# Third batch's shared down products moved to the closing stage, expert weights loaded in paced parts, odd sums as two additions

## What is computed

```python
h = _layernorm(x) * (1 + ca) + sa
x = x + ga * attention(h)                 # 16 heads of 16
h = _layernorm(x) * (1 + cb) + sb
# router: softmax over 32 experts, the best 4 per token, weights normalised
sh = silu(h @ shared_gate_w.T) * (h @ shared_up_w.T)         # 512 wide
out0 = sigmoid(h @ shared_expert_gate_w.T) * (sh @ shared_down_w.T)
# for each expert e: gate, up = h @ gate_up_proj[e].T (96 each)
#                    out += w_e * ((silu(gate) * up) @ down_proj[e].T)
x = x + gb * out
```

## Time and profile before

| what | value |
|---|---|
| median of 3 runs | 603.67 us (603.39 to 603.87) |
| the profiled execution | 604.01 us |
| its span | 602.2 us |
| granted TensorE clock, mean | 0.974 |
| PE, DVE, ACT, POOL busy | 94%, 62%, 42%, 36% |
| finish stage | about 334 to 408 us |
| expert loop on TensorE | 407.5 to 552.6 us |
| late and closing stages | 552.6 to 602.2 us |

### The profile page before, as it was taken

The page is one execution under the profiler, slowest core; times in us unless marked ns, Lnnn a source line. Parts: engine busy times, 40 slices in busy tenths (PEclk is TensorE's granted clock), DMA queues, the critical chain, the costliest instruction groups (busy, mean ns, idle before and its releaser), DMA issues.

```text
span 602.2 us, 10736 instructions
## 1 busy us (share of the span) xinstructions
PE 563.6 (94%) x3118; PEld 313.8 (52%) x3119; DVE 370.8 (62%) x860; ACT 255.3 (42%) x519; POOL 217.8 (36%) x284
## 2 busy tenths in 40 slices
PE   4889999999999999999999999998999999999881
PEld 3443233333333333333343465668888898897570
DVE  6385677778589785898855569435444444443683
ACT  3113545564765647555568140022343443433000
POOL 6100000000110751108434653441675666667332
PEclk9966999999999999999999999999999999999996
DMA  7242126100501224012101169524555645540791
GB/s 227 42 132 97 34 54 188 37 11 10 115 4 34 93 70 115 7 31 90 53 1 41 66 267 330 147 82 130 158 157 151 182 144 165 166 124 9 269 371 58
DMA packets 42343, 67.18 MB, mean 112 GB/s; under 512 B 9291, under 2 KB 32212, under 8 KB 41948
## 3 DMA queue, kind: packets, MB, share of 16 engines
q1 hardware_dynamic: 30208, 45.62, 25.9%
q0 software_dynamic: 7680, 16.87, 8.2%
q10 hardware_dynamic: 4416, 4.20, 2.1%
HBM read 38.93 MB, written 27.51 MB: 110 GB/s over the span
## 4 chain that ended last, share of the span: by engine, by line
PE 81%; DVE 8%; issue 3%; DMA 3%; SPq 1%; ACT 1%; POOL 1%; ACTq 0%; POOLq 0%; DVEq 0%
PE ps L863 23%; PE ps L876 10%; PE ps L1089 9%; PE ps L1110 6%; PE ps L960 6%; PE ps L812 5%; PE ps L954 3%; PE ps L834 3%; PE ps L1075 3%; PE ps L821 3%; PE ps L889 3%; DVE max_q L1201 2%; PE ps L1100 2%; PE ps L798 2%; PE ps L919 1%
## 5 line engine op out<-in xcount | busy, mean ns | idle before, releaser
L1201 DVE TENSOR_REDUCE max_q<-ps 128x1 f32<-128x512 f32 x256 | 163.8, 686 | 74.5 <-PE ps L834 72.8
L691 ACT ACTIVATE probs<-ps 128x512 f32<-128x512 f32 x256 | 138.0, 596 | 99.5 <-PE ps L863 99.2
L834 PE MATMUL ps<-k_rows,q_rows 31*128 31x512 f32 x512 | 149.7, 678 | 1.8 <-DMA k_rows<-qk_raw 1.8
L863 PE MATMUL ps<-q_rows,k_rows 32*128 32x512 f32 x512 | 147.6, 646 | 0.9 <-DVE max_q L1201 0.9
L545 POOL DMA_INDIRECT results<-y_sb,dest x96 | 94.5, 984 | 64.8 <-issue 35.0
L863 PEld LDWEIGHTS ps<-q_rows,k_rows 32*128 32x128 f32 x512 | 42.9, 186 | 71.6 <-ACT probs L691 52.2
L1089 PE MATMUL ps<-up_sb,oT 128*128 x384 | 70.7, 328 | 1.5 <-DVE oT L1565 1.3
L876 PE MATMUL ps<-probs,v_ext 128*32 128x512 f32 x512 | 68.2, 605 | 1.1 <-ACT probs L691 1.1
L1089 PEld LDWEIGHTS ps<-up_sb,oT 128*128 128x128 f32 x384 | 61.4, 191 | 2.1 <-issue 1.9
L1110 PE MATMUL ps<-down_sb,e_hidT 96*128 x192 | 49.8, 383 | 3.8 <-ACT e_hidT L748 3.8
L498 POOL TENSOR_TENSOR rstd<-veps,mhalf 128x4 f32<-128x4 f32 x4 | 4.1, 1036 | 134.3 <-DVE veps L1283 132.4
(11 more groups left out here) (180 smaller groups left out, 695.7 us busy)
## 6 DMA issues: line engine op xcount, KB each, us to landing
xe<-dispatched SPq DMA_DIRECT2D x96, 129.0 KB, 2.1
up_sb<-results SPq DMA_DIRECT2D x16, 512.0 KB, 7.9
up_sb<-in_up SPq DMA_DIRECT2D x2, 3072.0 KB, 15.1
dispatched<-pad_rows SPq DMA_DIRECT2D x33, 129.0 KB, 4.5
down_sb<-in_down SPq DMA_DIRECT2D x1, 3072.0 KB, 31.3
x<-in_x ACTq DMA_DIRECT2D x4, 512.0 KB, 5.1
q_rows<-qk_raw SPq DMA_DIRECT2D x64, 32.0 KB, 1.9
k_rows<-qk_raw SPq DMA_DIRECT2D x64, 32.0 KB, 1.9
```

Source lines behind the costliest of these rows:

```text
L691: act.activation(probs[:, u % 8, :], ps[:, st_bank(t.b, g, u), :], ACT.Exp).then_inc(exp_done, 1)
L834: pe.matmul(ps[:, banks[u % len(banks)], :], q_rows[32 * i:32 * i + ONE, b % 2, g, qt * P:(qt + 1) * P], k_rows[32 * i:32 * i + ONE, b % 2 ...
L863: pe.matmul(ps[:, st_bank(b, g, n), :], k_rows[32 * i:32 * i + 32, b % 2, g, kt * P:(kt + 1) * P], q_rows[32 * i:32 * i + 32, b % 2, g, :] ...
L1201: dve.tensor_reduce(max_q[:, g % 2, qt, i:i + 1], ps[:, banks[(16 * g + n) % len(banks)], :], AXX, ALU.max).then_inc(max_done, 1)
```

## The change

Four edits. (1) SD0@2 and SD1@2 leave the end of `Finish.shared` and stand at the head of `Late.shared`; TensorE does them before it waits for the last results, and `late_s`, on which GpSimd waits before it adds to batch 3's tiles, is still signalled only by batch 3's SD. (2) `comb` becomes a third layer of the overlay with 16 places, one a tile; SP issues the sixteen loads one after the other without waits. (3) The weights are loaded in 12 parts of `up` (512 KB) and 4 of `down` (768 KB); each part waits for the landing of the one before. The up parts no longer wait for the dispatches of batches 0 to 2, the down parts still do. (4) An odd tile's sum is an addition of two halves (512 columns) and one of two quarters (256 columns), in place in `comb`, instead of one reduction into `gtmp`; the waits for a free `gtmp` go.

```diff
-        self.shared += [f"SG0@{B - 1}", f"SG1@{B - 1}", f"SD0@{B - 2}", f"SD1@{B - 2}"]
+        self.shared += [f"SG0@{B - 1}", f"SG1@{B - 1}"]
...
-        self.shared = [f"SU0@{s}", f"SU1@{s}", f"SG2@{s}", f"SU2@{s}", f"SG3@{s}", f"SU3@{s}", f"SD0@{s}", f"SD1@{s}"]
+        self.shared = [f"SD0@{s - 1}", f"SD1@{s - 1}", f"SU0@{s}", f"SU1@{s}", f"SG2@{s}", f"SU2@{s}", f"SG3@{s}", f"SU3@{s}", f"SD0@{s}", f"SD1@{s}"]
...
-            [("up_sb", [P, KD * E * 2 * DM], F32), ("down_sb", [DM, E * D], F32)])
-        comb = up_sb[:, 0:CR * TOPK * D].rearrange("p (r n) -> p r n", r=CR)
+            [("up_sb", [P, KD * E * 2 * DM], F32), ("down_sb", [DM, E * D], F32)],
+            [("comb", [P, NT, TOPK * D], F32)])
...
+            parts = 0
+
+            def paced():
+
+                above(sp, up_ld, 16 * parts)
+
             sp.wait_ge(pv_done, 4 * NG * B)
+            n = E * 2 * DM // WP
+            for k in range(KD):
+                for w in range(WP):
+                    paced()
+                    sp.dma_start(up_sb[:, k * E * 2 * DM + w * n:k * E * 2 * DM + w * n + n],
+                                 up[k * P:(k + 1) * P, w * n:w * n + n]).then_inc(up_ld, 16)
+                    parts += 1
             for j in range(TJ):
                 sp.wait_ge(disp[j], 16 * TOPK * (B - 1))
-            for k in range(KD):
-                sp.dma_start(up_sb[:, k * E * 2 * DM:(k + 1) * E * 2 * DM],
-                             up[k * P:(k + 1) * P, :]).then_inc(up_ld, 16)
-            sp.dma_start(down_sb[:, :], down).then_inc(up_ld, 16)
+            n = E // 4 * D
+            for w in range(4):
+                paced()
+                sp.dma_start(down_sb[:, w * n:w * n + n], down[:, w * n:w * n + n]).then_inc(up_ld, 16)
+                parts += 1
...
-                if t >= CR:
-
-                    sp.wait_ge(part_s if t % 2 else sum_full, (t - CR) // 2 + 1)
-                sp.dma_start(comb[:, t % CR, :], yk[t * P * TOPK:(t + 1) * P * TOPK, :].rearrange(
-                    "(p k) d -> p (k d)", k=TOPK)).then_inc(comb_ld[t % CR], 16)
+                sp.dma_start(comb[:, t, :], yk[t * P * TOPK:(t + 1) * P * TOPK, :].rearrange(
+                    "(p k) d -> p (k d)", k=TOPK)).then_inc(comb_ld[t], 16)
...
-            pe.wait_ge(up_ld, 48)
+            pe.wait_ge(up_ld, 16 * (KD * WP + 4))
...
-            for name in late.shared[2:6]:
+            for name in late.shared[2:8]:
                 shared(name)
...
-                    if t is late:
+                    if t is late and s == B - 1:
                         dve.sem_inc(late_s, 1)
...
-            for name in late.shared[0:6]:
+            for name in late.shared[0:8]:
                 shared(name)
...
-                dve.wait_ge(comb_ld[odd % CR], 16 * (odd // CR) + 16)
-                if n >= 2:
-                    dve.wait_ge(prod_s, 2 * n - 2)
-                dve.tensor_reduce(gtmp[:, n % 2, :], comb[:, odd % CR, :].rearrange("p (k d) -> p d k", k=TOPK), AXX, ALU.add).then_inc(part_s, 1)
+                four = comb[:, odd, :]
+                dve.wait_ge(comb_ld[odd], 16)
+                st.then(dve.tensor_tensor(four[:, 0:2 * D], four[:, 0:2 * D], four[:, 2 * D:4 * D], ALU.add))
+                dve.tensor_tensor(four[:, 0:D], four[:, 0:D], four[:, D:2 * D], ALU.add).then_inc(part_s, 1)
                 dve.wait_ge(sum_full, n + 1)
                 gated_sum(2 * n, ps[:, n % 2, 0:D])
                 dve.wait_ge(part_s, n + 1)
-                gated_sum(odd, gtmp[:, n % 2, :])
+                gated_sum(odd, four[:, 0:D])
```

More of the change, by code:

```diff
@@ L31 @@
 CR = 8
+WP = 6
 class Steps:
@@ L159, in sem, with overlay @@
             return ctx.enter_context(nc.semaphore(name))
-        def overlay(first, second):
+        def overlay(*stages):
             made, ends = [], []
-            for specs in (first, second):
+            for specs in stages:
                 with ExitStack() as here:
@@ L168, in overlay @@
                     ends.append(nc.sbuf_base)
-            sb(f"{first[0][0]}_{second[0][0]}", [P, max(ends) - nc.sbuf_base], mybir.dt.uint8)
+            sb("_".join(specs[0][0] for specs in stages), [P, max(ends) - nc.sbuf_base], mybir.dt.uint8)
             return made
-        q_rows, k_rows, probs, v_ext, h2_even, mod_rows, up_sb, down_sb = overlay(
+        q_rows, k_rows, probs, v_ext, h2_even, mod_rows, up_sb, down_sb, comb = overlay(
             [("q_rows", [P, 2, NG, S], F32), ("k_rows", [P, 2, NG, S], F32), ("probs", [P, 2 * G, S], F32),
              ("v_ext", [P, 2, TJ, H, 32], F32), ("h2_even", [P, TJ, ROW], F32), ("mod_rows", [B, 4, D], F32)],
-            [("up_sb", [P, KD * E * 2 * DM], F32), ("down_sb", [DM, E * D], F32)])
-        comb = up_sb[:, 0:CR * TOPK * D].rearrange("p (r n) -> p r n", r=CR)
+            [("up_sb", [P, KD * E * 2 * DM], F32), ("down_sb", [DM, E * D], F32)],
+            [("comb", [P, NT, TOPK * D], F32)])
         wmod, gate_b, wo_sb, h2_odd, sh_tanh, onehot, picked, ex, rank, chosen, tabf, tab, cnt, past, past_n, h2T_late = overlay(
@@ L273, in adaln_moe_kernel @@
         y_out = [sem(f"y_out{i}") for i in range(YP)]
-        comb_ld = [sem(f"comb_ld{i}") for i in range(CR)]
+        comb_ld = [sem(f"comb_ld{i}") for i in range(NT)]
         part_s, sum_full, prod_s, x3_done, stored, late_s = (sem(n) for n in ("part_s", "sum_full", "prod_s", "x3_done", "stored", "late_s"))
@@ L1155, in _ @@
                     shared(f"SD{n - 2}@{B - 1}")
-                pe.wait_ge(comb_ld[t % CR], 16 * (t // CR) + 16)
+                pe.wait_ge(comb_ld[t], 16)
                 if n >= 2:
@@ L1160, in _ @@
                 for k in range(TOPK):
-                    mm = pe.matmul(ps[:, n % 2, 0:D], ident[:, :], comb[:, t % CR, k * D:(k + 1) * D], start=(k == 0), stop=(k == TOPK - 1))
+                    mm = pe.matmul(ps[:, n % 2, 0:D], ident[:, :], comb[:, t, k * D:(k + 1) * D], start=(k == 0), stop=(k == TOPK - 1))
                 mm.then_inc(sum_full, 1)
```

## The result

The changed kernel takes 609.66 us (median of 5 runs, 606.93 to 611.52) against 603.67: ratio 1.0095, 95% interval 1.0071 to 1.0119. It is slower by 6.0 us, where the prediction said 603.2 and a range of 600.3 to 606.0. The profiled execution took 608.77 us with a span of 607.0; before it was 604.01 and 602.2. Its lines are numbered 12 to 15 higher from L431 on.

The account below looks back on a forecast made before the run. TensorE, with 81% of the chain, was taken as the bound, so only seams and tail could move. Seam -5.0, late stage +5.4 and end -0.9 gave -0.5 us: 603.2 forecast, range 600.3 to 606.0.

Parts of the forecast that it names:

- The seam: Between finish stage and expert loop: with two down products moved away, the first widening comes at 405.2, a gain of 5.0 us.
- First xe load: At the seam, SP's first xe load leaves at 399.25 instead of 402.95, 3.7 us earlier.
- no stall of 9.7 us at the dispatches: Before the seam: small weight parts cure GpSimd's 9.7 us dispatch wait, so dispatches end about 9 us earlier.
- B: Rival, 15%: weights arrive late at the seam; up and down cycles of 4.3 and 6 us cost 5.5 us, 608.7.
- fourth down part issued by 398: Sign for the seam: SP issues the last down weight part by 398; the summed time was 396.5.
- The late stage: Behind the expert loop: the moved products add 6.9 us of TensorE work; sums begin 5.4 us later before the seam's gain.
- The closing stage: From first sum to GpSimd's last addition: 28.3 us instead of 29.2, a gain of 0.9.
- The turn-taking: In the last three rounds of sums, VectorE's and GpSimd's additions alternate: 2.8 us a round against 2.52.
- Rival A: 27%: cheaper additions in the closing sums; rounds of about 2.3 us give 601.7, 1.8 without turn-taking gives 600.2.
- part 2: The two down products in the late stage: sums begin at 564.85 against 564.44 after subtracting the seam's 5.0, +0.4 us.
- Rival C: 12%: TensorE's granted clock falls in the wait at the seam, costing 1.2 us, 604.4.
- D: Rival, 8%: the finish stage shifts by itself, GpSimd's products meet VectorE's routing chain later, up to 1 us, 604.2.

Follow-up runs that it names:

- f1_changed: The changed kernel run again as it is, beside the kernel before: 609.89 us, ratio 1.0093.
- g1: Changed kernel, but a pair buffer's reload waits for the result to leave PSUM, not for its scatter's landing; VectorE waits for that: 599.83 us, ratio 0.9921.
- f2: The kernel before with only the move of SD0@2 and SD1@2 to the late stage: 613.43 us, ratio 1.0148.
- f3_paced: The kernel before with only the paced weight loads: 605.76 us, ratio 1.0032.
- f4_closing: The kernel before with only the sixteen comb places and the two additions: 603.76 us, ratio 0.9996.
- g5_down_back: The changed kernel with SD0@2 and SD1@2 back in the finish stage: 604.58 us, ratio 1.0006 of the kernel before.
- g3_filler: The changed kernel with four extra unused matmuls on TensorE between its last shared gate and the expert loop: 606.75 us, ratio 1.0029 of the kernel before.
- g4_two: The changed kernel with two parts of the expert weights in flight instead of one: 609.88 us, ratio 1.0078 of the kernel before.

## Why the prediction was wrong

**The seam: right in its steps, 0.9 to 1.8 us short.** Summed 5.0, measured 4.16 in the first trace, of which 1.0 is luck (the attention ended early), and 1.64 in f1_changed; counted from the end of the attention it is 3.2 and 3.6, and 4.1 in g1. First xe load 399.49 (399.25 summed), fourth down part issued 397.91 (396.5), no stall of 9.7 us at the dispatches, the longest wait of L536 for a landing 1.2 us. Short was the load's landing: 3.47 us behind the last down part, which was still coming in, instead of the usual 2.1. With B's cycles of 3.9 and 5.7 us (medians of the page, against 3.7 and 5.45) B had a hand in it, at about 1 us, not at 5.5. In f1_changed the sign "fourth down part issued by 398" failed, as the second fence shows. But its parts had begun 3 us later with the attention (335.91 against 332.96) and took as long as in the first trace, and TensorE came 3 us later to the seam as well, so this is the whole program shifted and not B's slow cycles:

```profile
up_sb<-in_up SPq DMA_DIRECT2D x12, 512.0 KB, 3.9
...
down_sb<-in_down SPq DMA_DIRECT2D x4, 768.0 KB, 5.7
```
```profile
400.63 0.31 SPq L441 DMA_DIRECT2D down_sb<-in_down  x1
```

**The late stage: right.** 6.91 and 10.30 us of TensorE behind the loop, then the first sum, without a wait for the results; +5.42 against 5.4:

```profile
553.34 6.91 PE ps L966 x32
560.25 10.30 PE ps L972 x24
570.55 3.45 PE ps L1173 x16
```

**The closing stage: right, a little better.** 27.89 us against 28.3 summed and 29.21 before. The turn-taking is there, in the timeline of the last rounds, which answers to the earlier trace rows:

```profile
587.25 0.69 DVE L1619 TENSOR_TENSOR comb<-comb 128x512 f32<-128x512 f32 x1 [0.16 <-DVE x L1454]
...
591.55 1.91 POOL L566 TENSOR_TENSOR x<-x,y_sb 128x256 f32<-128x256 f32 x2 [0.76 <-DVE y_sb L1607]
...
591.66 1.21 DVE L1619 TENSOR_TENSOR comb<-comb 128x512 f32<-128x512 f32 x1
592.91 0.83 DVE L1620 TENSOR_TENSOR comb<-comb 128x256 f32<-128x256 f32 x1
...
594.33 1.21 DVE L1619 TENSOR_TENSOR comb<-comb 128x512 f32<-128x512 f32 x1
```

An addition alone takes 0.69 us, beside GpSimd 1.21, and GpSimd's pair takes 1.91 instead of 1.58. The round is 2.67 us (591.66 to 594.33): summed 2.8, and slower than the 2.52 of the reductions. f2, which has the move with the old reductions, gives the same account from the other side: 28.2 us from 570.58 to the end. So of the 1.3 us gained only 0.35 is that of the additions and the sixteen places; the other 1.0 is the waits for loads inside the sums, which went because the loads had landed before the first sum. Rival A is refuted.

**The loop: the failing step.** In part 2 the prediction subtracts the seam's 5.0 us from 569.9, as if the 142 us between passed every us on, because the earlier trace rows gave TensorE 81%. The loop has no term in the sum; it was put at nothing, and it measured +4.85 us (+4.00 in f1_changed). Its mechanism is the ring of g1: result, scatter (2.8 us of issue on GpSimd), landing (2.7 us usual), address work and two loads on SP (2.4), landing (2.1), transposition. By the records of before, pair 8's transposition to its result is 12.7 us (427.94 to 440.66), and pair 0's result to the landing of pair 8's load 10.1 (416.83 to 426.92): 22.8 us for one turn, against 22.6 for eight pairs of TensorE's. So there is next to no slack in which a delay can vanish: what falls into the ring once stays. The table of pairs gives the sizes: 0.7 us from pair 0 to 6, 3.3 from 6 to 8, 0.85 from 8 to 16, nothing after. Three things fell into the ring. The first, the scatter of pair 0, landed in 5.14 us; in the kernel before it took 2.7 (419.62 to 422.31). The queues in 417.5 to 420 us show an instruction fetch beside it:

```profile
q1 hardware_dynamic: 138, 0.13, 26.5%
q0 software_dynamic: 97, 0.23, 24.5%
q8 instruction: 1, 0.02, 4.7%
```

One packet is 4.7% of 16 engines over 2.5 us, 1.9 us of one engine; by the landing records all of the scatter but its last piece had landed at 419.39, and that one at 421.30. Ten traces bear on this, and they fall into two groups. The times are those of pair 0's second scatter, of the fetch packet on queue q8 nearest to it, and of the scatter's last landing:

| kernel | scatter issued | fetch, length | landed after its issue |
|---|---|---|---|
| before | 419.62 | 417.08, 1.11 | 2.69 |
| f3_paced | 422.52 | 419.93, 0.93 | 2.41 |
| f4_closing | 419.23 | 417.09, 0.93 | 3.23 |
| g5_down_back | 419.57 | 416.96, 1.11 | 2.42 |
| f2_move | 420.45 | 423.39, 1.46 | 3.06 |
| changed | 416.16 | 417.78, 1.90 | 5.14 |
| f1_changed | 419.01 | 420.43, 1.79 | 4.82 |
| g3_filler | 417.09 | 418.70, 1.32 | 4.53 |
| g4_two | 419.66 | 421.90, 0.93 | 4.34 |
| g1_early | 417.18 | 418.84, 1.60 | 4.86 |

In the last five, those with the move and the paced loads together, the fetch starts while the scatter is under way, and the scatter's last piece lands 1.2 to 1.6 us after the fetch's end, 1.6 to 1.9 us behind the rest of it. In the first four the fetch is over before the scatter is issued, in f2 it starts when the scatter has all but landed. So the earlier seam put the loop's first scatter ahead of the fetch, where it had been behind it. Four of the five lose 3.9 to 4.9 us in the loop; g1, whose loads do not wait for the scatter, has the late landing and doesn't lose by it. Second, the clock fell in the seam and, in the first trace, again behind the wait at 426.00. Third, there was a second late load at 448.61, of 3.68 us, with another fetch at 449.18. g1 and g3 show the ring and the clock to be causes: from the first widening of pair 0 to that of pair 8 it takes 21.89 us before, 25.92 changed and 21.78 in g1. That the fetch delays the scatter rests on these ten traces; no run moved the fetch alone.

A warning stood in the profile of before. Its own chain, read on past the 411 us where I stopped, leaves TensorE for a scatter and a load (437.66, 445.68) and returns at 449.50. That says that the loop is bound by the ring as well, though not that a gain ahead of it would be lost:

```profile
437.66 2.93 DMA results<-y_sb,dest
...
445.68 3.77 DMA xe<-dispatched
449.50 0.66 PE ps L1075 x4
```

**Rival C: right in kind, too small.** The clock fell in the wait that the freed seam leaves, as C said, and g3 puts the price at 3 us, not 1.2. That the rest comes from the ring, which passes the lost time on, is argued: the second fall is in one trace of the changed kernel and not in the other. B came in small. D's later products did not appear; what moved by itself was the end of the attention, by 1.0 us down and 2.0 up. The forecast went wrong on a term that no rival named. Even with that term at nothing the change would have gained next to nothing: -4.16, +5.42 and -1.32 are -0.1 us.

**The two rules of the Trainium skill.** DMA: Bandwidth & Descriptors, Queues, rings and completion order, says that an engine serves its queues in turn by whole packets. The fetch fits it: a single packet of 0.9 to 1.9 us, and one piece of the scatter that lands 1.6 to 1.9 us behind the rest. I had used the rule for the weight loads only. SBUF — State Buffer, Who interferes with whom, says in addition that a reduction does not contend with GpSimd while a sum of two SBUF inputs does; the additions' 1.21 us beside GpSimd against 0.69 alone, the reductions' 1.9 in both places, and a round of 2.67 against 2.52 agree. By that rule the additions are shorter by themselves and save no time where they meet GpSimd.

## What to carry to other kernels

Before a gain at the head of a loop is carried through it, read the chain inside the loop and close the ring of its buffers: if use, store, landing, reload and landing take as long as the turn, the loop is bound by both, and an earlier start need not be an earlier end. Look then for what a reload waits for that it doesn't need; here a wait moved from the scatter's landing to the result's leaving PSUM brought 9.8 us where the kernel before takes 604 (at 652 and 658 us it brought the kernel before nothing). And compare two executions of one kernel before a figure of one is called a gain: the first widening came 4.16 us earlier in one and 1.64 in the other. And work taken out of a seam is a gain only if the next things are ready: the move alone, without the paced loads, gained nothing there (410.47 against 410.45) and cost its 5.4 us behind.

## What the runs showed of the hardware

- TensorE stalled for 1.1 to 1.2 us once in each turn of an unrolled loop where the loads led their use at the turn by 0.6 to 1.5 us (before), and for 0.0 to 0.4 where they led by 2.4 to 6.3 (g1).
- An instruction fetch is one packet of 0.9 to 1.9 us on one DMA engine. A scatter in whose flight it fell landed in 4.34 to 5.14 us (five traces); where it was over before, or began 0.1 us before the landing (f2), 2.4 to 3.2 (five traces).
- The kernel before stood at 604 us three times and at 652 to 658 three times, partly on a chip of the same number. The changed kernel without the move stood at 1.0006 and 1.0007 of it in the two; loosening the loads brought the kernel before nothing at 652 and 658, and wasn't measured at 604.
- A 768 KB load of 96 partitions landed in 5.7 us, a 512 KB load of 128 partitions in 3.9 (medians of the changed kernel's page, one part at a time).
